# Queries, keys and attention by token halves, with the next row's first norm moved into the FFN

## The reference, cut to what matters

```python
x = x + mamba2_mixer(layernorm(x), ...)   # 32 heads x 64, state 128, conv 4, sequential scan over 512 tokens
x = x + bitlinear_ffn(layernorm(x), ...)  # sigmoid(x1) * x2, 704 hidden, ternary weights
x = x + attention(layernorm(x), ...)      # 16 heads x 16, ALiBi and causal mask, softmax(q k^T / 4 + bias) v, W_o
x = x + moe(layernorm(x), ...)            # router of 64 experts, top 6 of 4 groups, capacity 64 over all tokens, plus a shared expert
```

## Time and profile before

| | |
|---|---|
| time, median of 3 runs | 1400.0 us (1399.84 to 1404.95) |
| profiled execution: span | 1398.3 us, so 1.7 us below the median of the runs |
| PE, DVE, ACT, POOL busy | 1163.0, 908.5, 655.5, 586.1 us |
| mean granted TensorE clock | 0.928 of full speed |
| period of one batch row | about 302 us (scores begin at 562.96 us in row 1 and at 1166.17 us in row 3) |

### The profile page before, as it was taken

How to read it: one execution, slowest core, us unless ns; L and a number is a source line. 1 busy time by engine, 2 the same in 40 slices (tenths; PEclk the granted TensorE clock), 3 DMA queues, 4 the chain that set the end, 5 groups by cost and what they waited for, 6 DMA issues and landing times.

```text
span 1398.3 us, 24417 instructions
## 1 busy us (share of the span) xinstructions
PE 1163.0 (83%) x8422; PEld 748.5 (54%) x8422; DVE 908.5 (65%) x1814; ACT 655.5 (47%) x1544; POOL 586.1 (42%) x789
## 2 busy tenths in 40 slices
PE   3799988798899977998899977989999886979940
PEld 2355556565565555664555655655555664644520
DVE  4488875555878766556888765656888755571417
ACT  3655523565455523657444334656545234620630
POOL 1255561220387742210677822210777711225760
PEclk9899999799999999899999997989999998989975
DMA  7366633700243314501333236101433529166879
GB/s 306 115 191 188 199 106 87 91 3 19 85 136 114 109 56 80 61 3 33 117 121 111 97 87 72 21 20 42 125 120 121 176 72 133 36 223 232 158 130 365
DMA packets 107499, 159.56 MB, mean 114 GB/s; under 512 B 11633, under 2 KB 68593, under 8 KB 106737
## 3 DMA queue, kind: packets, MB, share of 16 engines
q1 hardware_dynamic: 92592, 129.64, 35.4%
q0 software_dynamic: 9216, 19.98, 5.5%
q10 hardware_dynamic: 5568, 8.39, 1.7%
HBM read 104.55 MB, written 40.83 MB: 104 GB/s over the span
## 4 chain that ended last, share of the span: by engine, by line
PE 48%; DVE 19%; POOL 11%; issue 9%; ACT 8%; DMA 3%; ACTq 1%; SPq 0%; POOLq 0%; DVEq 0%
PE bank L1067 12%; DVE pool_c L1537 5%; PE bank L1109 4%; PE bank L992 4%; PE bank L1225 3%; POOL joint L1998 3%; PE bank L1249 3%; DVE joint L1553 3%; PE bank L1264 2%; POOL xn L2005 2%; PE bank L1088 2%; PE bank L1103 2%; PE bank L1337 2%; PE bank L1207 2%; PE bank L1096 2%
## 5 line engine op out<-in xcount | busy, mean ns | idle before, releaser
L1067 PE MATMUL bank<-xnT,joint 128*128 128x512 f32 x544 | 274.6, 629 | 20.8 <-DVE pool_c L1537 15.6
L1998 POOL TENSOR_TENSOR joint<-joint 128x512 f32<-128x512 f32 x128 | 168.6, 1318 | 244.7 <-DVE joint L1553 244.1
L1537 DVE SCALAR_TENSOR_TENSOR pool_c<-bank,params,pool_c 128x511 f32<-128x511 f32 (+2 forms) x216 | 161.3, 747 | 85.9 <-ACT pool_c L716 80.4
L1067 PEld LDWEIGHTS bank<-xnT,joint 128*128 128x128 f32 x544 | 100.3, 198 | 125.2 <-issue 93.8
L1708 DVE TENSOR_REDUCE nmax<-bank 128x1 f32<-128x512 f32 (+3 forms) x176 | 109.9, 639 | 74.6 <-PE bank L1226 73.4
L755 ACT ACTIVATE joint<-bank,dt_ 128x64 f32<-128x64 f32 x512 | 112.1, 343 | 27.8 <-PE bank L992 27.7
L1109 PE MATMUL bank<-wout,pool_c 128*128 128x256 f32 x512 | 123.4, 384 | 1.2 <-DVE pool_c L1578 1.2
L1109 PEld LDWEIGHTS bank<-wout,pool_c 128*128 128x128 f32 x512 | 97.3, 193 | 35.3 <-issue 23.3
L1992 POOL DMA_INDIRECT xslot<-xrow,slots x96 | 97.2, 1013 | 34.9 <-issue 20.3
L857 ACT ACTIVATE pool_c<-bank 128x512 f32<-128x512 f32 (+1 forms) x176 | 91.4, 549 | 37.0 <-PE bank L1251 35.4
L725 ACT ACTIVATE pool_c<-pool_c 128x512 f32<-128x512 f32 x64 | 40.3, 629 | 135.9 <-DVE pool_c L1537 135.9
(11 more groups left out here) (266 smaller groups left out, 2419.1 us busy)
## 6 DMA issues: line engine op xcount, KB each, us to landing
pool_b<-dA_rows SPq DMA_DIRECT2D x64, 256.0 KB
pool_b<-dec_rows SPq DMA_DIRECT2D x96, 128.0 KB, 3.7
joint<-pool_b SPq DMA_DIRECT2D x96, 128.0 KB, 8.6
acc<-xrow SPq DMA_DIRECT2D x13, 640.0 KB, 6.5
joint<-dA_rows SPq DMA_DIRECT2D x32, 256.0 KB, 3.3
dA_late<-dA_rows SPq DMA_DIRECT2D x32, 256.0 KB, 4.1
xslot<-xrow SPq DMA_DIRECT2D x16, 321.0 KB, 4.7
pool_b<-xslot SPq DMA_DIRECT2D x64, 80.2 KB
```

The source lines that it names most:

```text
L1067: last = mm(bank[:, :], win[:, k, col:col + P], xnT[:, k, :], start=(k == 0), stop=(k == KD - 1))
L1537: ins = v.scalar_tensor_tensor(out=cv[:, n:L], in0=bank[:, 0:L - n], scalar=convw[:, ci, TAPS - 1 - n:TAPS - n], in1=cv[:, n:L], op0=ALU.m ...
L1998: M_ready.inc(p.tensor_tensor(M[u % 2][:, hs_, :], Lx[:, hs_, :], cbm[:, c * P:(c + 1) * P].unsqueeze(1).to_broadcast([P, 4, P]), ALU.mult))
```

## The change

- Q and k are projected, split and copied by token halves. The first half's q and k products (`queries_keys(0, e)`, e = half of the heads) run in the FFN's steps n = 11 and 12; v of the first half, then q and k of the second half follow; the last of them (`queries_keys(1, 1)`, `project_values(1)`) run inside attention. The split works on 256 columns (`split`, `finish_split`).
- The 24 copies by DMA stay 24 of the same size, but each takes 8 heads and 256 tokens (runs of 512 bytes in place of 1024), from 128 source partitions in place of 64, to 16 partitions that lie six apart (`BROWS + i:ROWS:PIECES`) in place of 16 neighbouring ones.
- Attention goes through the tiles in order, all four head quarters of t = 0, then t = 1, 2, 3. `turn outputs`, `project` and `normalize` of the first token half stand in the middle of the list in place of its end. Transposed scores take banks 5 and 6, with bank 7 as a third only in t = 3.
- The next row's norm 0 has its own buffers and signals (`hstats`, `hmv`, `hrstd`, `xm`, `head_*`). Its statistics stand in DVE's mixer end, its roots in POOL's, its four `norm_apply` in FFN steps 0 to 3, its transposes in PE's steps 6 and 8, its two copies on ACT after steps 7 and 9. x of the next row is loaded in the mixer (after u = 5). `step_products` follows v of the first half.
- In the FFN both up-products of a step share one bank (`up_part`), the sigmoid waits for both, and the down-products of two tiles share a bank (`down_part`).

```diff
-AGROUPS = [(t, q) for q in range(2) for t in range(T)] + [(t, q) for t in range(T) for q in (2, 3)]
+AGROUPS = [(t, q) for t in range(T) for q in range(AH // AQ)]
...
+        attention_steps.insert(0, ("split", 2))
+        after(attention_steps, ("max", 1), 0, ("finish split", 2))
+        after(attention_steps, ("max", 1), 1, ("late queries", 1))
+        after(attention_steps, ("max", 1), 2, ("next", 0))
+        after(attention_steps, ("max", 4), 0, ("split", 3))
+        after(attention_steps, ("max", 5), 0, ("finish split", 3))
+        after(attention_steps, ("max", 6), 0, ("late values", 1))
+        after(attention_steps, ("max", 7), 0, ("next", 1))
+        after(attention_steps, ("max", 11), 0, ("next", 2))
+        after(attention_steps, ("turn", 7), 1, ("turn outputs", 0))
+        after(attention_steps, ("turn outputs", 0), 4, ("project", 0))
+        after(attention_steps, ("project", 0), 4, ("normalize", 0))
...
+        def score_bank(n):
+            return (5, 6)[n % 2] if n < first_of_block[3] else (5, 6, 7)[(n - first_of_block[3]) % 3]
...
 # SP
+                for p_ in range(2):
+                    cols = slice(p_ * HALF, (p_ + 1) * HALF)
+                    for e in range(2):
+                        sp.wait_ge(part3.sem, part3.upto(2 * (2 * p_ + e) + 2, b))
                         for i, (qp, kp) in enumerate(zip(QPARTS, KPARTS)):
-                            r0, kp = BROWS + i * AD, kp + 3
-                            stacked[q].inc(sp.dma_start(qks[r0:r0 + AD, q * AQ:(q + 1) * AQ], four[:, qp:kp + 1:kp - qp, :]))
+                            kp = kp + 3
+                            stacked[2 * p_ + e].inc(sp.dma_start(qks[BROWS + i:ROWS:PIECES, e * EH:(e + 1) * EH, :, cols],
+                                                                 parts[e][:, qp:kp + 1:kp - qp, cols]))
...
 # ACT, FFN
+                    if coming is not None and n in (FT + 1, FT + 3):
+                        row(coming)
+                        norm_copy(0, n // (FT + 3))
+                        row(here)
+                    if n == FT + 4:
+                        norm_copy(2, 0)
...
 # PE
+                    if coming is not None and n in (FT, FT + 2):
+                        row(coming)
+                        norm_T(0, (n - FT) // 2)
+                        row(here)
+                    if n == FT + 3:
                         norm_T(2, 0)
+                    if n >= FT + 5 and n < FT + 7:
+                        queries_keys(0, n - FT - 5)
+            def second_queries(coming):
+                here = b
+                project_values(0)
+                if coming is not None:
+                    row(coming)
+                    normed(0)
+                    step_products()
+                    row(here)
+                norm_T(2, 1)
+                queries_keys(1, 0)
+                if coming is not None:
+                    pe.wait_ge(dt_abs.sem, dt_abs.upto(1, coming))
...
 # DVE, end of the mixer
+                    if coming is not None:
+                        row(coming)
+                        ...
+                        for t in range(2 * p_, 2 * p_ + 2):
+                            norm_stats(0, t)
+                        row(here)
                     for t in range(2 * p_, 2 * p_ + 2):
                         norm_apply(1, t)
...
 # DVE, after the FFN
+            def first_queries(coming):
+                here = b
+                split(0)
+                finish_split(0)
                 for t in range(2, T):
                     add_ffn(t)
                     norm_stats(2, t)
+                split(1)
+                norm_apply(2, 2)
+                finish_split(1)
+                norm_apply(2, 3)
+                if coming is not None:
+                    row(coming)
+                    step_sizes()
+                    row(here)
...
 # POOL, end of the mixer
                     norm_rstd(1, [2 * p_, 2 * p_ + 1])
+                    if coming is not None:
+                        row(coming)
+                        norm_rstd(0, [2 * p_, 2 * p_ + 1])
+                        row(here)
```

More of the change, by code:

```diff
@@ L398, in build, with after @@
             attention_steps.insert(min(i + 6, len(attention_steps)), ("turn", g))
[L399 to L408 removed]
+        def after(steps, step, n, new):
+            steps.insert(min(steps.index(step) + 1 + n, len(steps)), new)
+        attention_steps.insert(0, ("split", 2))
[10 more added lines that the diff above has]
+        after(attention_steps, ("project", 0), 4, ("normalize", 0))
+        last_steps = list(attention_steps)
+        after(last_steps, ("normalize", 0), 3, ("apply", 0))
+        after(last_steps, ("apply", 0), 3, ("turn norm", 0))
+        at_normalize = attention_steps.index(("normalize", 0))
+        maxima_before_norm = sum(all(attention_steps.index(("max", n)) < at_normalize for n in ns) for ns in of_group)
         of_pair_done = [max(g for g, (t, _) in enumerate(AGROUPS) if t // 2 == p) + 1 for p in range(2)]
@@ L807, in ffn @@
[L807 to L821 removed]
+                    hh_done.inc(sa.activation(hh[:, f, p_ * HALF:(p_ + 1) * HALF], hid[n % 2][:, 0:HALF], ACT.Copy))
@@ new lines, in ffn, with split @@
+                    if coming is not None and n in (FT + 1, FT + 3):
[4 more added lines that the diff above has]
+                        norm_copy(2, 0)
+            def split(j):
+                at(qk_mm, 2 * j + 2)
+                for m in range(2):
+                    bank, part = split_of(j, m)
+                    part1.inc(sa.activation(part[:, 0, :], bank, ACT.Copy, scale=scale_of(m)))
@@ L841, in attention @@
                             at(o_mm, n - 1)
-                        oT_done.inc(sa.activation(oT[n % 2], pb[4 + n % 2][:, 0:P], ACT.Copy))
+                        oT_done.inc(sa.activation(oT[n % 2], outputs_of(n), ACT.Copy))
+                    elif step == "split":
+                        split(n)
+                    elif step == "finish split":
+                        finish_split(n)
+                    elif step == "late values":
+                        take_values(n)
                     elif step == "rows":
@@ L948, in _ @@
                 mixer_steps()
-                ffn()
-                qkv()
-                if coming is not None:
-                    row(coming)
-                    for p_ in range(2):
-                        norm_copy(0, p_)
-                    row(r)
+                ffn(coming)
+                first_queries()
                 warm(ACT.Exp)
@@ L1308, in attention @@
                         norm_T(3, n)
+                    elif step == "late queries":
+                        queries_keys(1, n)
+                    elif step == "late values":
+                        project_values(n)
                     elif step == "next" and n == 2 and coming is not None:
+                        at(v_done, 2)
                         row(coming)
@@ L1421, in _ @@
                 mixer_steps()
-                ffn()
-                qkv()
-                if coming is not None:
-                    at(qk_rest, 4)
-                    row(coming)
-                    for p_ in range(2):
-                        norm_T(0, p_)
-                    normed(0)
-                    step_products()
-                    row(r)
+                ffn(coming)
+                second_queries(coming)
                 attention(coming)
```

360 lines of the change are left out of this document (202 added, 158 removed).

## The result

Before 1399.9 us (1399.25 to 1404.95), after **1378.3 us** (1377.96 to 1379.56, 4 runs each); ratio 0.9837, 95% interval 0.9823 to 0.9851. That is 21.6 us less, where 31.1 were forecast; the time lies in the forecast's own range (1358 to 1380).

A forecast was written before the change was run, and what follows sets the result against it. PE was taken as the bound, with idle waits ahead of attention. Rows 0 to 2 gain 7.2 us each (21.6), row 3 gains 9.5: 31.1 off 1400.0 gives 1369 us, own range 1358 to 1380 (0.58), 8-in-10 range 1352 to 1388.

The forecast's parts named there:

- the banks': In attention, two banks instead of three for transposed scores: ACT's row copy felt about twice a row, +1.0 us a row.
- Head norm: Mixer's end and FFN, rows 0 to 2: `rms` 2.0 us late, FFN ends 3.5 us later; bounds 1.4 to 5 us.
- q and k in the FFN: Row 3's FFN: hid of n = 11 at 1144.4, not 1143.14; first six copies issued at 1148.5, not 1157.13.
- Copies: Before attention: six copies take SP's 4.2 us plus 2.8 landing; scores 9.4 us earlier in row 1, 9.8 in row 3.
- the rival: Copies of q and k keep 129 GB/s; gain falls by 12.4 us to give 1381 us; chance 0.10.
- Attention: First score to last values, by tiles: added PE work, start and banks less the clock's 3.8, +2.2 us; bounds -2 to +9.
- The start: Attention's first t = 0 groups: PE has 2.3 us of gaps against 0.95 before, +1.4 us.
- Tail: Last row, up to the router: first half's output product and norm are done before the last values, -1.9 us.
- the clock falls again: At attention's start, t = 0 groups leave PE a quarter idle; 3.8 us return in each row, 1384 us; chance 0.11.

## Why the prediction was right, and its gain 9 us too high

Each part of the sum but the banks' shows in the profile, and the time lies in the forecast's own range, near its upper end. By the medians the gain was 9.5 us less than forecast (21.6 for 31.1), by the profiled executions 9.0. Step by step:

1. **Head norm.** `rms` 1.87 us late against 2.0; confirmed by moving the roots, in the trace (0.90 us wait again). The FFN's own delay can be read where the clock is kept up, in the run with the FFN's end filled: the last hidden product of DVE comes 23.8 us after the first up-product in rows 0 to 2, where it was 20.6 to 20.9 before. That is 2.9 to 3.2 us for the 2.7 of steps 1 and 2 (1.4 for the four applications, 1.3 for the transposes and the copy).
2. **q and k in the FFN.** In row 3 the last hidden product of DVE comes at 24.1 us after the first up-product, not at the forecast's 21.9 (1144.4 less 1122.5). PE waits for `norm_T(2, 0)`, 2.62 us in rows 0 to 2 and 3.65 in row 3, and then forms products of the last steps at the half clock in rows 0, 2 and 3; in row 1 the clock stayed up. With the waits filled the 24.1 are 23.2, so 0.9 us of the 2.2 are the clock's and 1.3 are a delay that the forecast had too small. This term was mis-sized, by 3.3 us in row 3 up to the scores, of which the fillings return 2.3.
3. **Copies.** Issue-bound as forecast: 2.4 us to land. That the partitions written set the rate was right, and the alternative (19 us for rows side by side) is dearer than the rival said (12.4). The runs show that the rows decide, and not by what means. The rule of the Trainium skill (SBUF — State Buffer, Door 1: The DMA port swizzle), that the bandwidth goes by the ports that the partitions reach, agrees with them: 8.4 to 2.5 us for the same copy. The about 109 GB/s that the Trainium skill gives there for 16 neighbouring partitions are somewhat under the 123 measured here. By the Trainium skill's map the new rows reach 13 ports in four of the six copies and 14 in two, not 13 in all, which changes nothing here.
4. **Attention.** +2.8, +2.8, +2.7, +1.4 us against +2.2. Its parts were less exact than their sum: PE's busy time grew by 1.0 (3.6 added, so 2.6 given back by the clock, not 3.8), and its idle time by 1.8, of which 1.47 is the wait for DVE's `normalize`, which the prediction had left out (it lets `normalize` "move but stay as long"; DVE's step stands between two maxima there, and cut in two it gives 0.9 us a row back). The start was sized right: PE's waits of over 0.25 us in the first 12 us sum to 2.2 us, and 2.3 were forecast. The 1.0 us for two banks is not seen: the waits for ACT's row copies are 0.7 us, 0.6 before. Waits of PE in row 1's attention after, by releaser (us in total, times, longest):

```profile
PE bank L1349 <- POOL mparts L2207: 1.5, 4, 0.6
PE bank L1340 <- DVE nmax L1851: 1.5, 1, 1.5
PE bank L1381 <- ACT pool_c L953: 0.9, 1, 0.9
```

5. **Tail.** +1.5 against +1.9.
6. **What was missing** is one thing for the most part: the clock. The prediction asked whether it would fall at the start of attention, as in the kernel before, and gave 1384 us to that case. It stayed up there, at 1.00 in all four rows. The reason given was that PE's gaps ahead of attention were now under 2 us each; yet in rows 2 and 3 q and k (1, 0) ran at the half clock behind just such gaps (0.55 and 0.69 us in row 2, 1.63, 0.55 and 0.69 in row 3). But it took the clock as given everywhere else, and it fell ahead of q and k (1, 0), at the FFN's last steps, and for longer in the router's products. Filling just those waits returned 7.9 and 5.5 us, together more than the 9.5 that were missing, since part of it had been lost before the change too. So the clock accounts for most of what is missing, and the rest is in steps 2 and 4; the runs don't split it more finely. The rival "the clock falls again" had the right mechanism at the wrong place.

## What to carry to other kernels

A step taken out of one wait leaves smaller waits, and each of them can cost the clock in work that nobody changed: after such a change read the granted clock over the whole row, not only where the edit is. Idle-time products in a spare bank gave 7.9 and 5.5 us here, where PE itself was late next; ahead of work that another engine paces they gave nothing, and that run lost 6.2 us elsewhere. And where a copy by DMA waits, look first at which partitions it writes: with the rows side by side this whole change was worth nothing that could be measured.

## What the runs showed of the hardware

- Six-apart rows in place of 16 neighbouring ones: 2.5 us to land instead of 8.4 for 128 KB in 1 KB pieces, 2.4 for 512-byte pieces. Into neighbouring rows they moved 123 GB/s with pieces of either size (row 3 of the kernel before, row 1 of the kernel after with its rows put back), and the median to landing, 8.4 or 5.8 us, went with how many were issued in one run. Into rows six apart, in the kernel before, they moved 197 GB/s (1159 to 1174), as fast as SP issued them.
- The same wait of PE (2.31 us) was followed by a mean clock of 0.81 in one kernel and 0.62 in another over 9 us: where the clock falls depends on more than that one wait.
